# Plain attention with keys masked by bands once, in fp32, for both score products

## What is computed

```python
q, k, v = heads(x_norm @ Wq + bq), heads(c @ Wk + bk), heads(c @ Wv + bv)   # L2a: c is x_norm
s = q @ k.T / sqrt(8)                # L0, L2a causal; L3 rotary, window of 64; L1, L2b unmasked
o = softmax(s) @ v                   # then @ Wo + bo and the residual
```

## Time and profile before

| | us |
|---|---|
| median of 3 runs | 3347.18 (3345.81 to 3347.89) |
| span of the profiled execution | 3447.8 |
| TensorE busy in it | 2817.4 |
| VectorE busy | 1989.0 |
| ScalarE busy | 1326.8 |
| GpSimd busy | 635.1 |

### The profile page before, as it was taken

One profiled execution on the slowest core, in us unless ns is written; L12 is line 12 of the kernel. 1 busy time (PEld: TensorE's weight loads), 2 busy tenths in 40 slices (PEclk: granted clock), 3 DMA queues, 4 the chain that ended last, 5 costly groups with the idle time before them and its releaser, 6 DMA issues.

```text
span 3447.8 us, 64821 instructions
## 1 busy us (share of the span) xinstructions
PE 2817.4 (82%) x24730; PEld 1996.0 (58%) x24818; DVE 1989.0 (58%) x6643; ACT 1326.8 (38%) x3062; POOL 635.1 (18%) x847
## 2 busy tenths in 40 slices
PE   5788988766687987988988988988988988987953
PEld 2344766634574864764764764755755755656743
DVE  2566444456544455666666666666766766765532
ACT  2343434433474743333333333334334334334521
POOL 0122112322312011121121121121111111111043
PEclk7888999877898998998998999998999999998977
DMA  7300647400373700000000000000000000003454
GB/s 254 113 23 22 199 129 208 131 19 22 125 229 99 240 23 7 3 9 7 3 9 7 3 9 7 3 9 7 3 9 7 3 9 4 3 4 112 130 168 147
DMA packets 146658, 217.14 MB, mean 63 GB/s; under 512 B 20392, under 2 KB 99248, under 8 KB 146224
## 3 DMA queue, kind: packets, MB, share of 16 engines
q1 hardware_dynamic: 134064, 187.80, 17.8%
q0 software_dynamic: 12288, 25.19, 2.4%
HBM read 159.83 MB, written 53.08 MB: 62 GB/s over the span
## 4 chain that ended last, share of the span: by engine, by line
PE 58%; DVE 21%; ACT 10%; issue 5%; another core or an unknown queue 2%; SPq 2%; DMA 1%; POOL 1%; DVEq 0%; POOLq 0%; ACTq 0%
PE bank L447 5%; PE bank L383 5%; ACT ex L1153 5%; PE bank L540 4%; PE bank L622 4%; DVE mx L1615 4%; PE bank L548 4%; PE bank L389 3%; PE bank L604 3%; PE bank L467 3%; PE bank L457 3%; PE bank L451 3%; PE bank L436 3%; PE bank L374 2%; PE bank L430 2%
## 5 line engine op out<-in xcount | busy, mean ns | idle before, releaser
L1153 ACT ACTIVATE ex<-bank 128x512 f32<-128x512 f32 x896 | 472.1, 600 | 692.7 <-PE bank L457 456.7
L1615 DVE TENSOR_REDUCE mx<-bank 128x4 bf16<-128x512 f32 x640 | 407.6, 684 | 133.2 <-PE bank L436 68.9
L965 POOL TENSOR_TENSOR rstd<-vare,power 128x2 f32<-128x2 f32 x192 | 136.1, 709 | 1377.9 <-DVE vare L1406 1377.9
L1032 POOL TENSOR_TENSOR oT<-oT 128x128 f32<-128x128 f32 x256 | 118.3, 462 | 916.2 <-DVE oT L1734 915.6
L540 PE MATMUL bank<-qm,expert 128*128 128x128 f32 x1872 | 260.2, 283 | 16.9 <-DMA expert<-in_moe 9.3
L974 POOL DMA_INDIRECT sent<-tail_tok,pos x192 | 192.0, 1000 | 394.0 <-DVE pos L1543 349.9
L383 PE MATMUL bank<-hT,wproj 128*128 128x256 f32 x736 | 242.8, 426 | 25.2 <-DVE oT L1734 8.5
L1607 DVE RECIPROCAL rden<-bank 128x16 f32<-128x16 f32 x160 | 41.1, 257 | 384.9 <-PE bank L476 347.1
L447 PE MATMUL bank<-qm,kf 32*128 32x512 f32 x1280 | 211.4, 723 | 57.1 <-ACT ex L1153 36.2
L540 PEld LDWEIGHTS bank<-qm,expert 128*128 128x128 f32 x1872 | 237.0, 198 | 28.6 <-DMA expert<-in_moe 15.5
L622 PEld LDWEIGHTS bank<-ev,ex 128*128 128x128 f32 x2048 | 247.6, 193 | 5.2 <-issue 0.4
(11 more groups left out here) (208 smaller groups left out, 5064.8 us busy)
## 6 DMA issues: line engine op xcount, KB each, us to landing
expert<-in_moe SPq DMA_DIRECT2D x78, 578.0 KB
expert<-in_moe SPq DMA_DIRECT2D x78, 512.0 KB
expert<-in_moe SPq DMA_DIRECT2D x78, 384.0 KB
sent<-zeros SPq DMA_DIRECT2D x8, 2560.0 KB, 12.8
ex<-sent SPq DMA_DIRECT2D x234, 64.0 KB
answered<-qm SPq DMA_DIRECT2D x234, 64.0 KB
ctxT<-ctx_kept SPq DMA_DIRECT2D x32, 128.0 KB
wproj<-in_wproj SPq DMA_DIRECT2D x1, 3072.0 KB
```

The source lines that it names most:

```text
L1153: give(nc.scalar.activation(ex[s][:, i], ps[:].rearrange("p (i q) -> p i q", i=4), ACT.Exp, scale=SCALE), *key)
L1615: give(nc.vector.tensor_reduce(mx[s][:, b, HB * i:HB * i + HB], ps[:].rearrange("p (i k) -> p i k", i=HB), AX.X, ALU.max), *k, "s", b, i)
```

## The change

ScalarE writes four masked copies of the keys in fp32 (`masked_keys`), at the step at which it copied the keys once, and one plain fp32 copy of the queries. VectorE's split of the keys stays for L3 alone and writes fp32; its query split and its bf16 copy go. The first score product reads the upper halves of the fp32 words of queries and keys as bf16. The transposed scores multiply each masked copy of the keys with the plain queries: 16 products of 128 columns where there were 4 of 512. TensorE waits for the two banks to be given back (`taken`) in place of two semaphores, in all but L3. The buffer `km` takes the place of `qm` under its other names, and `t_out` gets memory of its own. Three planned delays are shorter and one longer.

```diff
-        qb = two("qb", [P, NT], BF16)
-        qm, km = two("qm", [P, HB, NT]), two("km", [P, HB, NT], BF16)
+        km = two("km", [P, HB, NT])
...
+        t_out = two("t_out", [P, OUT_SLOTS, P])
...
+        km_bf16 = [km[s][:].rearrange("p h n -> p (h n)").bitcast(BF16)[:, 1::2].rearrange("p (h n) -> p h n", h=HB)
+                   for s in range(STREAMS)]
+        qf_bf16 = [qf[s].bitcast(BF16)[:, 1::2] for s in range(STREAMS)]
...
-                        if b == j == 0:
+                        if b == j == 0 and rot:
                             pe.wait_ge(sem[f"keys_ready{s}"], w.next(f"keys_ready{s}"))
                             pe.wait_ge(sem[f"queries_ready{s}"], w.next(f"queries_ready{s}"))
+                        elif b == j == 0:
+                            if own_keys:
+                                taken(*k, "k")
+                            taken(*k, "q")
...
-                            mm = nc.tensor.matmul(ps[i][:], qb[s][r, seq(b)], km[s][r, :, seq(b)], start=True,
+                            mm = nc.tensor.matmul(ps[i][:], qf_bf16[s][r, seq(b)], km_bf16[s][r, :, seq(b)], start=True,
...
-                        for j in range(BANDS):
-                            nc.tensor.matmul(ps[j][:], kf[s][band_rows(j), seq(b)], qm[s][band_rows(j), :, seq(b)],
-                                             start=True, stop=False)
+                        for i in range(HB):
+                            for j in range(BANDS):
+                                nc.tensor.matmul(ps[j][:, i * P:(i + 1) * P], km[s][band_rows(j), i, seq(b)],
+                                                 qf[s][band_rows(j), seq(b)], start=i == 0, stop=False)
...
-                    yield "q", 0.9 if rot else 0.45, 3.0 if rot else 2.0
+                    yield "q", 0.9 if rot else 0.45, 2.2 if rot else 0.8
...
-                    yield "q", 1.35, 2.5
-                    yield from attend(k, 0, tail=tail)
+                    yield "q", 1.35, 3.0
+                    yield from attend(k, 0, tail=tail, own_keys=False)
...
-                    yield "q", 0.45, 2.0
+                    yield "q", 0.45, 0.8
...
+                def masked_keys(src, bias):
+                    for h in range(HB):
+                        if bias is None:
+                            ins = nc.scalar.activation(km[s][:, h, :], src, ACT.Copy, scale=band[:, h:h + 1])
+                        else:
+                            ins = nc.scalar.activation(km[s][:, h, :], src, ACT.Identity, bias=col(f"{bias}{h}"),
+                                                       scale=band[:, h:h + 1])
+                    return ins
...
                 def queries(k, name, bias, rot=False, keys_too=False):
                     ps = take(*k, "q")
+                    ins = shifted(qf[s][:], ps[:, 0:NT], name if bias else None)
                     if rot:
...
+                        ins = shifted(qs[s][:], ps[:, NT:2 * NT], name + "s")
                     if keys_too:
...
+                        ins = masked_keys(ps[:, NT:2 * NT], None)
                     give(ins, *k, "q")
...
-                        nc.vector.tensor_copy(qb[s][:], qf[s][:]).then_inc(sem[f"queries_ready{s}"], 1)
+                        rotate(qf).then_inc(sem[f"queries_ready{s}"], 1)
...
-                    if rot:
-                        split(qm, qf).then_inc(sem[f"split_ready{s}"], 1)
```

More of the change, by code:

```diff
@@ L83 @@
     "rstd_ready",
-    "split_ready",
     "keys_ready",
@@ L279, in build @@
                      for s in range(STREAMS)]
-        eq = [[qm[s][:, 0:2, :], qm[s][:, 2:4, :], qfs[s][:]] for s in range(STREAMS)]
+        eq = [[km[s][:, 0:2, :], km[s][:, 2:4, :], qfs[s][:]] for s in range(STREAMS)]
         ek = [two(f"ek{i}_", [P, NT]) for i in range(3)]
@@ L1937, in laid_out @@
     in_band = np.arange(P)[:, None] % 32 // D == np.arange(HB)[None, :]
-    for n in ("L0q", "L1q"):
+    for n in ("L0k", "L1k"):
         for h in range(HB):
```

55 lines of the change are left out of this document (14 added, 41 removed).

## The result

| | before | after |
|---|---|---|
| median, run side by side, us | 3347.53 (3345.81 to 3348.49) | 3381.67 (3378.5 to 3384.37) |
| ratio, 95% interval | | 1.0091 (1.0069 to 1.0112) |
| span of the profiled execution, us | 3447.8 | 3376.6 |

The changed kernel is 34 us, 0.9%, slower. So the two profiles can't be set against each other span by span: something other than the change differs between these two executions as well. The experiments take that up.

A forecast was written before the change was run, and what follows sets the result against it. No engine alone bounds the kernel; TensorE is fullest (82% busy) and loses time waiting for VectorE and ScalarE. Terms -22 - 35 + 16 + 0 + 4 = -37 us of span, times 0.971 is -36: 3311 us, range 3262 to 3355.

The forecast's parts named there:

- second rival: Behind the key projection, ScalarE's key copies end on the path and TensorE stalls: 40 us lost, 3386 us; chance 0.08.
- The query copies: Behind the query projection, one copy instead of five frees the PSUM bank sooner: 22 us gained, ends 0 and 44.
- VectorE's split and copy: VectorE loses 97.0 us of key splits, query splits and bf16 copies; 35 us gained on the path, ends 0 and 97.
- the key copies on ScalarE: Four masked key copies replace one in L0, L1, L2b: 61 us more work, 16 us lost, ends 0 and 61.
- The transposed scores on TensorE: 16 small products replace four, weight loads hidden: 1.06 us a phase against 1.14, taken as 0; good end 13 us.
- third rival: In the transposed scores each reload waits for its own band: 1.96 us a phase for 1.14, 3401 us; chance 0.10.
- The first score product: It reads bf16 halves out of fp32 words, every second element, instead of packed bf16: no cost, 0.
- The order: Shorter planned delays put the first unit behind the query projection more often: 4 us lost; third-stage reordering 0, 15 both sides.
- The base: Sum made on the profiled span, 3447.8 us; gains counted at 0.971 for the runs' median of 3347.18 us.

The follow-up runs named there:

- early bank: Kernel before with one plain fp32 query copy, bank given back behind it, masked copies made from SBUF, order kept: 3321.21 us (0.9912), again 3325.82 us (0.9926).
- i2: The changed kernel as it is, run again beside a kernel before of 3427.91 us: 3511.77 us, ratio 1.0225.
- e3: Kernel before with its transposed scores as 16 products of 128 columns, nothing else changed: 3492.52 us, ratio 1.017.
- g1: Kernel before with GpSimd's 192 indirect scatters replaced by plain DMAs to fixed rows: 3374.9 us, ratio 0.9808.
- f1: Changed kernel with GpSimd's 192 indirect scatters replaced by plain DMAs to fixed rows: 3405.68 us, ratio 0.9902 to the kernel before.

## Why the prediction was wrong

The forecast was 3311 us, the result 3382. The second rival had 3386, which is near by luck: its mechanism, key copies that end on the path, isn't what the runs show. In the order of the steps:

- **The query copies** (22 us gained, ends 0 and 44): right. Alone, with the 4.7 us copy of VectorE in them, they gave 30 and 24 us in two 3350 us jobs, and L430's waits for qm are gone.
- **VectorE's split and copy** (35 us), **the key copies on ScalarE** (16 us lost): together 19 us were to be gained. The changed engines in the old order gained 28 us more than the early bank beside them (3298.0 against 3325.8). Nothing in the runs shows the 16 us lost on ScalarE: TensorE's own waits for the key masks are 5.0 us in all, and its idle time that ends on ScalarE is no longer than with the early bank. The second rival falls with it. The 28 us weren't split between the two terms by a run.
- **The transposed scores on TensorE** (0): right for the phase, 1.106 us against 1.073. The third rival had 1.96 us and falls. The Trainium skill's rule in "TensorE: Matmul & The Clock Gate", "Part 3: Packing small matmuls", that a weight load overlaps only a matmul of another row group, isn't borne out by this: each band is reloaded for each of its four products, and the 160 phases are 5 us longer in all. But the term had no entry for the instruction stream. Its queue has 30 packets more (230 for 200), and in a 3430 us job the 16 products cost 58 us. In the job of the result this counts little: the idle time of TensorE that is put down to issue sums to 4.7 us over its lines there, and to 40.9 in i2. No run has the 16 products alone in a 3350 us job.
- **The first score product** (0): right as far as the runs show it; nothing in them needs a cost here.
- **The order** (+4, with 15 us on both sides): this is the step that failed. In its words, "the rest of the reordering in the third stage has no row to price it; I take 0 and put 15 us on both sides." It is 84 us in the 3350 us jobs, 90 in one 3430 us job, 56 on the engines of before, and 59 of the 79 us of span lie in that third stage. In place of nothing the third part, with the end, lost 53 us: 32 of longer busy time of TensorE, of which more work at 1.2 GHz makes 19 by the estimate above, and 21 of idle time. I had looked for places where scores follow their own query projection, and priced the copy that they wait for (0.61 us). That part is true: the waits for qfs are 10.8 us, 8.6 of them in L0, against 2.8 with the old delays. But L0 lost 21 us, so even where there was a row to price it the term was too small. I hadn't looked for where all eight score products stand in a row, though the order of the instructions shows it without a run, nor at how the two streams come to stand against each other. Nor had I counted that idle time can be followed by work at half the clock.
- **The base.** The profile of before was of a 3430 us job and the median of a 3350 us one. I scaled by 0.971, as if all work were slower by the same share. It wasn't: a part of the difference sat in idle time put down to issue, of which TensorE has 40.8 us in the profile of before and 4.7 in that of after. In the sum the factor moves only 1 us; what it hid is that the rows came from the other kind of execution.

Without the order the forecast would have been 40 us under before (the sum of -41 times 0.971), and the same kernel in the old order measured 52. So in a 3350 us job the sum of the engines' terms was right and a little undersized, and the sign was lost to three numbers in the planner. In the 3430 us jobs the same kernel stood between 6 us under and 10 us over the kernel before, so there the engines' gain didn't show. What stays open is where the rest of the order's cost sits, and why the new order costs the engines of before 56 us and those of the change 77 to 90.

## What to carry to other kernels

A change of planned delays is a change of its own: measure it apart from the work that it comes with, and read in the instruction order where products stand in a row that is longer than their ring of buffers. Judge a wait on TensorE by its idle time and by the clock of the work behind it. And when one wait has grown, add up all of TensorE's idle and busy time before you call it the cause: here it grew by 20 us while another shrank by as much. If a profile's span isn't that of the timed runs, find out what differs before any gain is scaled from one to the other.

## What the runs showed of the hardware

In the 3430 us jobs TensorE falls idle beside GpSimd's indirect DMAs without an engine that it waits for: in e3 and i2 matmuls come in lots of 2 to 6 with 0.2 to 0.3 us between, at a granted clock of 1.00 (789 to 793 us in i2), and in e3 gaps of 0.8 and 1.0 us follow. Such idle time beside the 192 scatters sums to between 16 and 49 us in the profiles of these jobs, to 0.9 to 3.4 us in those of the 3350 us jobs with the same scatters, and to 0.9 to 3.9 us with plain sends. Plain sends in their place save 65 us in the kernel before and 115 us in the changed one (g1, f1), and with the scatters the 16 products, 32 matmul records in a phase for 8, cost 58 us instead of 1.5. That it is the fetch of the instruction stream is inferred from the idle time's form and from the queue's packets, 230 for 200; no run measured the fetch itself. The same program differs between jobs by more than this idle time: the changed kernel spans 3376.6 us and, in i2, 3509.9, and 36 of these 133 us are idle time put down to issue. It goes with the chip as far as five jobs tell: one chip had 3440 and 3428 us for the kernel before, another 3434, two more 3351 and 3350. What the chips differ in wasn't found.
